# The second routed layer as one list of 47 tiles, with the shared expert behind its first nine

## The chip, the cores and the metric

The kernel runs on one core of a Trainium2 chip. The metric is device time in microseconds, the median of the runs: 534.43 us for the kernel before (three runs, 534.42 to 536.74). One instruction stream each drives PE (TensorE), ACT (ScalarE), DVE (VectorE), POOL (GpSimd) and SP (SyncE); they meet only at semaphores. SP's queue and POOL's queue start the DMAs.

## The reference

The input is four batches of 512 tokens of width 256: 2048 tokens, 16 tiles of 128. Half a routed feed-forward layer is added, then attention, then half of the same feed-forward layer once more.

```python
def _L0_ffn_ref(hidden_states, gate_w, expert_bias, ...):      # 16 experts, two per token
    scores = jax.nn.sigmoid(router_logits)                      # x @ gate_w
    _, selected = jax.lax.top_k(scores + expert_bias[None, :], K)
    top_scores = top_scores / (top_scores.sum(-1, keepdims=True) + 1e-20)
    shared = jax.nn.silu(x @ shared_gate_w) * (x @ shared_up_w) @ shared_down_w
    for e in range(E):
        gu = x @ experts_gate_up[e]
        g, u = jnp.split(gu, 2, axis=-1)
        routed = routed + comb[:, e:e + 1] * (jax.nn.silu(g) * u @ experts_down[e])
    return (shared + routed).reshape(b, s, h)
...
    x = x + 0.5 * _L0_ffn_ref(_layernorm(x, axis=-1), ...)      # FFN 1
    x = x + _L0_attn_ref(_layernorm(x, axis=-1), ...)           # per batch, 3 heads, all 512 x 512 scores
    x = x + 0.5 * _L0_ffn_ref(_layernorm(x, axis=-1), ...)      # FFN 2
```

## The kernel before

The whole x stays in SBUF (`x_sb`), and so do all weights. Each fp32 product is made of three passes over a high and a low part, so ACT copies a high part out of PSUM and DVE subtracts to get the low part.

A token goes to two experts. In FFN 2 the 4096 (token, expert) pairs lie in DRAM in `slab_dram`, one slab of rows for each expert. POOL writes them there with indirect DMAs (`slab_row`, L1879), one DMA for 128 tokens and one of their two choices. A tile is 128 rows of one slab. SP loads it (`load_row`, L2045), PE turns it (`turn`, L396), multiplies by the expert's gate and up weights (six matmuls), ACT takes silu (L1006), DVE multiplies (L1577), PE turns the result (L657), PE multiplies by the down weights (three matmuls) and ACT copies the output out (L1017); SP stores it to `y_dram` (L2072). `ffn` runs this as a pipeline: in step s, PE turns tile s, does gate and up of tile s-1, turns the hidden rows of tile s-3 and does the down product of tile s-4. Four row buffers hold loaded tiles. So SP can load tile n once tile n-4 has been turned.

A list of tiles must be known before SP and PE can index. DVE computes it from the counts of each expert (`tile_table`), PE brings it into one row (`pack_table`), DVE writes it (`write_table`), and SP and PE load registers from it. Attention runs batch by batch, and the routing of batches 0 to 2 is done beside it. Batch 3 is ready only when attention ends. So FFN 2 has two lists: one for batches 0 to 2, up to 39 tiles, and one for batch 3, up to 23 tiles; 62 steps that are always run. After each list's rows SP writes zeros behind each slab (`clear_rest`, L2057, 16 DMAs each time), so that the unused lanes of a last tile hold zeros.

Beside the steps of FFN 2, `late_front` on each engine does the routing of batch 3 (turns, router product, sigmoid, choice, ranks, slab addresses, eight slab stores) and brings batches 0 to 2 back: SP reloads their normed rows from `xn_dram`, PE turns 12 tiles (`return_tile`, L461), ACT and DVE split them. Those are the inputs of the shared expert, which is done for all four batches after the last tile (`shared_gu`, `shared_y`).

Last, POOL gathers each token's two outputs from `y_dram` (`gather_pair`, L1869, 32 indirect DMAs), DVE adds them into `x_sb` with their weights (`combine`, L1492), DVE adds the shared expert's output (`shared_sink`, L1258), and SP stores the output (`tail2`, L2109). The order on each engine is the order in which the code is written; there is no scheduler.

## Time and profile before

| | |
|---|---|
| median of 3 runs | 534.43 us (534.42, 534.43, 536.74) |
| span of the profiled execution | 536.0 us |
| PE, PEld, DVE, ACT, POOL busy | 466.7, 414.9, 350.9, 280.6, 255.1 us |
| attention's last matmuls end, first tile of FFN 2 is turned | 394.96 us, 396.24 us |
| last down product of FFN 2 ends | 510.89 us |

The page gives the profiled execution no time of its own besides its span. The span lies between the lowest and the highest of the three runs. "Idle before" names what an engine waited for and for how long. A group of rows with "x2" is two instructions whose spans may overlap.

### The profile page before, as it was taken

What the parts mean: (1) busy time and instruction counts of PE and PEld (TensorE: products, weight loads), DVE (VectorE), ACT (ScalarE), POOL (GpSimd) and SP (SyncE); (2) the same over time, 40 slices, a digit from 0 to 9 for tenths busy, and PEclk for the clock granted to TensorE, in tenths of its full rate; (3) what the DMA queues carried; (4) which work ended last, traced back from release to release, by engine and by line L of the source; (5) the groups of instructions that cost most, each with busy time, mean ns of one, the idle gap of its engine ahead of it and who ended that gap; (6) DMA issues with size and microseconds to landing.
All of it is one profiled execution on the core that took longest, in us unless ns stands there. A gap on an engine that the chain in (4) does not pass through costs nothing.

```text
span 536.0 us, 10796 instructions
## 1 busy us (share of the span) xinstructions
PE 466.7 (87%) x3155; PEld 414.9 (77%) x3155; DVE 350.9 (65%) x1048; ACT 280.6 (52%) x763; POOL 255.1 (48%) x262
## 2 busy tenths in 40 slices
PE   1566799999777999999999999999888999899985
PEld 1335688999666989988898988899777888898874
DVE  5469675565457655387466756756648677678766
ACT  3765266676533445445444544454446866566621
POOL 4357775565064753474337557373740022026571
PEclk9987599999999999999999999999989999999999
DMA  8743445665631200011002111030545477758755
GB/s 296 246 127 117 138 140 179 196 207 135 163 91 59 60 1 0 21 51 39 11 1 59 41 41 50 10 109 11 181 126 181 158 224 235 224 167 252 213 150 178
DMA packets 52263, 65.49 MB, mean 122 GB/s; under 512 B 7056, under 2 KB 45456, under 8 KB 52208
## 3 DMA queue, kind: packets, MB, share of 16 engines
q1 hardware_dynamic: 44928, 46.02, 26.8%
q0 software_dynamic: 6864, 18.75, 12.9%
q8 instruction: 29, 0.48, 0.4%
q14 instruction: 26, 0.21, 0.1%
q10 hardware_dynamic: 416, 0.02, 0.1%
HBM read 36.33 MB, written 28.44 MB: 121 GB/s over the span
## 4 chain that ended last, share of the span: by engine, by line
PE 43%; DVE 8%; DMA 6%; issue 4%; ACT 3%; SPq 2%; POOL 1%; DVEq 0%; ACTq 0%
PE bank L390 38%; DMA stage<-slab_dram 4%; PE bank L396 3%; DVE x_sb L1492 1%; DVE softmax_row L1743 1%; PE bank L420 1%; PE bank L657 1%; ACT v_sp L1143 1%; DVE x_sb L1603 1%; SPq L2072 1%; DVE v_sp L1757 1%; DVE raw L1194 1%; DMA late_pair<-y_dram,slot_i 1%; DVE stats L1175 0%; POOL e_sp L1957 0%
## 5 line engine op out<-in xcount | busy, mean ns | idle before, releaser
L1957 POOL TENSOR_TENSOR e_sp<-raw,e_sp 128x512 fp32r<-128x512 f32 x48 | 62.3, 1298 | 72.1 <-ACT e_sp L1114 71.7
L390 PE MATMUL bank<-v_sp,e_sp 128*128 128x256 f32 x576 | 77.2, 284 | 2.0 <-DVE x_sb L1603 1.9
L390 PEld LDWEIGHTS bank<-v_sp,e_sp 128*128 128x128 f32 x576 | 74.3, 191 | 5.7 <-issue 2.7
L390 PE MATMUL bank<-g_sp,xT 128*128 128x512 f32 x288 | 74.8, 395 | 0.1
L390 PE MATMUL bank<-w_hi,e_sp 128*128 (+1 forms) x234 | 62.5, 293 | 2.4 <-DVE e_sp L1242 1.0
L390 PE MATMUL bank<-w_hi,xt_late 128*128 x248 | 61.8, 311 | 0.6 <-DVE xt_late L1572 0.5
L1924 POOL DMA_INDIRECT raw<-xn_dram,gather_at x47 | 46.2, 983 | 31.7 <-PE bank L396 28.8
L390 PEld LDWEIGHTS bank<-g_sp,xT 128*128 128x128 f32 x288 | 51.7, 189 | 9.4 <-issue 0.2
L1135 ACT ACTIVATE raw<-bank,softmax_row 128x512 f32<-128x512 f32 x48 | 33.2, 692 | 48.6 <-DVE softmax_row L1743 48.2
L1568 DVE TENSOR_TENSOR e_sp<-bank,e_sp 128x128 fp32r<-128x128 f32 x109 | 31.5, 289 | 30.9 <-ACT e_sp L987 30.1
L1743 DVE TENSOR_REDUCE softmax_row<-bank 128x1 f32<-128x512 f32 x48 | 32.9, 685 | 28.1 <-PE bank L390 27.8
L1869 POOL DMA_INDIRECT late_pair<-y_dram,slot_i x32 | 31.0, 969 | 39.0 <-DMA y_dram<-raw 24.0
L390 PE MATMUL bank<-b_sp,xT 128*128 128x256 f32 x288 | 44.0, 289 | 5.1 <-DVE v_sp L1757 4.9
L390 PEld LDWEIGHTS bank<-w_hi,e_sp 128*128 128x128 f32 x234 | 43.9, 189 | 5.5 <-issue 3.2
L1006 ACT ACTIVATE raw<-bank 128x128 f32<-128x128 f32 x109 | 30.4, 279 | 32.8 <-PE bank L390 32.6
L1757 DVE SCALAR_TENSOR_TENSOR v_sp<-bank,softmax_row,v_sp 128x256 fp32r<-128x256 f32 x48 | 23.2, 484 | 35.9 <-ACT v_sp L1143 35.9
L390 PE MATMUL bank<-w_hi,xT 128*128 x188 | 46.1, 307 | 0.6 <-DVE xT L1572 0.5
L390 PEld LDWEIGHTS bank<-w_hi,xt_late 128*128 128x128 f32 x248 | 44.2, 196 | 1.6 <-issue 1.2
L390 PEld LDWEIGHTS bank<-b_sp,xT 128*128 128x128 f32 x288 | 38.0, 191 | 7.4 <-DVE v_sp L1757 6.9
L1862 POOL DMA_INDIRECT stage<-y_dram,slot_i x32 | 32.3, 1010 | 22.4 <-DMA y_dram<-stage 14.6
L1577 DVE TENSOR_TENSOR raw<-raw,bank 128x128 f32<-128x128 f32 x109 | 31.2, 286 | 15.1 <-ACT raw L1006 10.7
L390 PE MATMUL bank<-xT,a_sp 128*128 128x512 f32 (+1 forms) x156 | 36.0, 379 | 0.8 <-DVE xT L1512 0.7
(247 smaller groups left out, 1123.3 us busy)
## 6 DMA issues: line engine op xcount, KB each, us to landing
stage<-slab_dram SPq DMA_DIRECT2D x62, 128.0 KB
y_dram<-raw SPq DMA_DIRECT2D x62, 128.0 KB, 2.7
y_dram<-stage SPq DMA_DIRECT2D x47, 128.0 KB, 2.6
slab_dram<-stage SPq DMA_DIRECT2D x32, 128.0 KB
stage<-in_w_pack SPq DMA_DIRECT2D x6, 384.0 KB, 5.4
raw<-in_w_pack SPq DMA_DIRECT2D x6, 384.0 KB, 3.4
x_sb<-in_x SPq DMA_DIRECT2D x4, 512.0 KB, 7.8
xn_dram<-xn_all SPq DMA_DIRECT2D x4, 512.0 KB, 4.6
```

The source lines that it names most:

```text
L390: m = pe.matmul(dst, lhs[k][l], rhs[k][r], start=(first and k == 0 and i == 0), stop=(last and k == n - 1 and i == 2), skip_group_check=True)
L396: m = pe.transpose(dst[:, k * P:(k + 1) * P], src[:, k * P:(k + 1) * P], ident[:])
L1006: act.activation(h_buf[:, g % 2, :], bank[GU_BANKS[g % 2]][:, 0:F], ACT.Silu).then_inc(s_silu, 1)
L1135: act.activation(e32[:, i, :], bank[S_BANKS[i]][:], ACT.Exp, bias=row_max[:, i, :], accum_out=row_sum[:, i, :]).then_inc(s_exp, 1)
L1568: dve.tensor_tensor(ht_rows[:, v % 2, 1], bank[HT_BANK][:, 0:P], ht_rows[:, v % 2, 0].bitcast(F32), ALU.subtract).then_inc(s_hT_lo, 1)
L1577: dve.tensor_tensor(h_buf[:, g % 2, :], h_buf[:, g % 2, :], bank[GU_BANKS[g % 2]][:, F:GU], ALU.mult).then_inc(s_act, 1)
L1743: dve.tensor_reduce(row_max[:, i, :], bank[S_BANKS[i]][:], AX, ALU.max, negate=True).then_inc(s_max, 1)
L1757: dve.scalar_tensor_tensor(out=v_sp[:, i, 1, :], in0=bank[V_BANK][:, 0:H], scalar=row_inv[:, i, :], in1=v_sp[:, i, 0, :].bitcast(F32), op0 ...
L1862: pool.indirect_dma_start(pair_buf[:, n % PAIRS, :], None, y_dram[0:NI * P, :], at).then_inc(s_pair[n % PAIRS], 16)
L1869: pool.indirect_dma_start(late_pair[:, n % LATE_PLACES, :], None, y_dram[0:(SPLIT_TILE if t < LATE_T else TILES[1]) * P, :], at).then_inc( ...
L1924: pool.indirect_dma_start(row_buf[0][:, n % ROWS, :], None, xn_dram, bass.IndirectOffsetOnAxis(ap=gather_at[:, n:n + 1], axis=0)).then_inc ...
L1957: pool.tensor_tensor(e_sp[:, i, 1, :], e32[:, i, :], e_sp[:, i, 0, :].bitcast(F32), ALU.subtract).then_inc(s_e_lo, 1)
```

## The change

One list takes the place of two. The first nine tiles are full tiles of batches 0 to 2: of their 3072 pairs at most 16 x 127 can lie outside full tiles, whatever the routing, so at least nine tiles are full, and these need neither zeros nor batch 3. Then the shared expert of all four batches is done, two of its gate and up products within steps 9 and 10 of the nine tiles, the rest after them. Then 38 tiles follow that hold all that is left, 47 in all. `slab_dram` has one slab per expert, with room for all batches, and zeros are written once (17 DMAs).

Rows of `slab_dram` are 272 floats wide instead of 256: the 257th holds the number of the pair (choice and token), written by POOL into the source before each slab store (`mark`). POOL reads it back from each loaded tile (`keep_id`) and scatters the tile's output straight to the place of the pair in `pair_dram` (`scatter_y`), instead of SP's store to `y_dram`. SP then loads both outputs of 128 tokens with one plain DMA (`load_pair`), instead of two gathers. SP may load tile n only after `keep_id` of tile n-4. `combine` is no longer spread over the steps: all 32 stand behind FFN 2 on DVE.

The inputs of the shared expert for batches 0 to 2 are no longer turned a second time: SP stores the turned tiles that the router used (`xT_dram`) and loads them back (`reload_batch`), ACT copies the high part and POOL subtracts (`back_hi`, `back_lo`, 128x1024 each), batch 0 in attention's last batch and batches 1 and 2 in FFN 2's first steps. The routing of batch 3 stands earlier by some steps, and the weights of all batches are computed in the later steps of the second part.

```diff
+    FULL_TILES = (LATE_T * TOPK * P - E * (P - 1)) // P + 1
+    EARLY_TILES = LATE_T * TOPK + E - 1
+    TILES = (NI, NI)
     BASE = (0, NI)
-    DONE = (NI, NI + TILES[1])
-    STEPS = tuple(n + LAG for n in TILES)
-    SLAB_TILES = (LATE_T + 1, TB + 1)
-    SLAB = sum(SLAB_TILES) * P
-    SLAB_LATE = SLAB_TILES[0] * P
-    TABLE = ((0, 40, 40), (80, 104, 24))
-    LATE_PLACES = 8
-    PAIRS_FROM = 44
+    DONE = (NI, NI + NI)
+    STEPS = (NI + LAG, NI + LAG)
+    ROW = H + 16
+    SLAB = T + P
...
+    y_put_value = [pairs_read[j % PAIRS] + 16 * (j // PAIRS + 1) for j in range(NI)]
...
-            shared_gu(1, 0)
-            for b in range(B):
-                if b + 1 < B:
-                    shared_gu(1, b + 1)
-                shared_y(1, b)
+            ffn(1, late_front, 0, FULL_TILES)
+            shared_y(1, 0)
+            shared_gu(1, 2)
+            pack_table(True)
+            shared_y(1, 1)
+            shared_gu(1, 3)
+            shared_y(1, 2)
+            shared_y(1, 3)
+            ffn(1, lambda s: None, FULL_TILES)
...
+            def back_hi(b):
+                x = front_x[1][b]
+                act.wait_ge(s_back[b], 16)
+                act.copy(x[:, 0], x[:, 1].bitcast(F32)).then_inc(s_back_hi, 1)
...
+            def late_shared(s):
+                if s == 10:
+                    shared_mul(1, 0)
+                elif s == 11:
+                    shared_lo(1, 0)
+                elif s == 12:
+                    shared_mul(1, 1)
+
+            def late_weights(s):
+                if s == FULL_TILES + 8:
+                    run(routing_weights(1, 0, LATE_T))
+                elif s == FULL_TILES + 16:
+                    run(routing_weights(1, LATE_T, NT))
...
-            ffn(1, between2)
-
-            for t in range(EARLY_COMBINED, LATE_T):
-                combine(1, t)
-            shared_mul(1, 0)
-            shared_lo(1, 0)
-            shared_mul(1, 1)
+                late_shared(s)
+
+            ffn(1, between2, 0, FULL_TILES)
             shared_lo(1, 1)
+            write_table(True)
             shared_sink(1, 0)
-            combine(1, LATE_T)
             shared_mul(1, 2)
-            combine(1, LATE_T + 1)
             shared_lo(1, 2)
             shared_sink(1, 1)
             shared_mul(1, 3)
-            combine(1, LATE_T + 2)
             shared_lo(1, 3)
-            combine(1, LATE_T + 3)
             shared_sink(1, 2)
             shared_sink(1, 3)
+            ffn(1, late_weights, FULL_TILES)
+            for t in range(NT):
+                combine(1, t)
...
+            def mark(rows, n, new):
+                nonlocal marked
+                if new:
+                    pool.memset(rows[:, H + 1:], 0.0).then_inc(s_mark, 1)
+                pool.tensor_copy(rows[:, H:H + 1], pair_id[:, n:n + 1]).then_inc(s_mark, 1)
+                marked += 2 if new else 1
+                pool.wait_ge(s_mark, marked)
...
+                if k == 1:
+                    pool.wait_ge(s_slab[t % TB], 16 * (t // TB * TOPK + 1))
+                mark(src, k * NT + t, k == 0 and (t < TB or t >= LATE_T))
...
+            def back_lo(b):
+                x = front_x[1][b]
+                pool.wait_ge(s_back_hi, b + 1)
+                pool.tensor_tensor(x[:, 1], x[:, 1].bitcast(F32), x[:, 0].bitcast(F32), ALU.subtract).then_inc(
+                    s_back_lo, 1)
+
+            def keep_id(j):
+                pool.wait_ge(s_row_late[j % ROWS], row_value(j))
+                row = row_buf[1][:, j % ROWS, :]
+                pool.tensor_scalar(tile_id[:, j % (TOPK * NT):j % (TOPK * NT) + 1], row[:, H + 1:H + 2], float(j),
+                                   row[:, H:H + 1], ALU.mult, ALU.add).then_inc(s_id, 1)
+
+            def scatter_y(j):
+                pool.wait_ge(s_y_copy, BASE[1] + j + 1)
+                pool.wait_ge(s_id, j + 1)
+                pool.indirect_dma_start(pair_dram, bass.IndirectOffsetOnAxis(
+                    ap=tile_id[:, j % (TOPK * NT):j % (TOPK * NT) + 1].bitcast(U32), axis=0), y_buf[1][:, j % Y_BUFS, :], None).then_inc(
+                        s_pair[j % Y_BUFS], 16)
...
-            pool.wait_ge(s_row_norm, NT + TB)
-            for t in range(LATE_T, NT):
-                for k in range(TOPK):
-                    pool.wait_ge(s_xt, BASE[1] + SCATTER_FROM + SCATTER_EVERY * ((t - LATE_T) * TOPK + k))
+            for j in range(ROWS):
+                keep_id(j)
+            back_lo(1)
+            keep_id(4)
+            scatter_y(0)
+            keep_id(5)
+            scatter_y(1)
+            back_lo(2)
+            keep_id(6)
+            scatter_y(2)
+            keep_id(7)
+            keep_id(8)
+            scatter_y(3)
+            for k in range(TOPK):
+                for t in range(LATE_T, NT):
                     slab_row(t, k)
-            for t in range(NT):
-                gather_pair(1, t)
+            for j in range(4, FULL_TILES):
+                scatter_y(j)
+            for s in range(FULL_TILES, NI + LAG):
+                if s < NI:
+                    keep_id(s)
+                if s - LAG >= FULL_TILES:
+                    scatter_y(s - LAG)
...
                 if n >= ROWS:
                     sp.wait_ge(s_xt, BASE[1] + n - ROWS + 1)
+                    sp.wait_ge(s_id, n - ROWS + 1)
                 sp.dma_start(row_buf[1][:, n % ROWS, :], slab_dram[bass.ds(rows["at"][i % PER_LOAD], P), :]).then_inc(
                     s_row_late[n % ROWS], 16)
...
+            def load_pair(t):
+                if t in (0, LATE_T):
+                    for i, value in enumerate(put_by(EARLY_TILES if t == 0 else NI)):
+                        sp.wait_ge(s_pair[i], value)
+                if t == 0:
+                    sp.wait_ge(s_ssink, 2 * B + 8)
+                sp.dma_start(late_pair[:, t], pair_rows[t]).then_inc(pairs_loaded[t][0], 16)
...
+            rows = {}
+            for n in range(ROWS):
+                load_row(n, rows)
+            reload_batch(1)
+            reload_batch(2)
+            for n in range(ROWS, FULL_TILES):
+                load_row(n, rows)
+            clear_rest()
+            for n in range(FULL_TILES, NI):
+                load_row(n, rows)
+            for t in range(NT):
+                load_pair(t)
```

POOL, from the end of attention on, before. `slab_dram<-stage` are slab stores, `e_sp` the low part of attention's exponentials, `late_pair` the gathers.

```order
L1957 TENSOR_TENSOR e_sp<-raw,e_sp 128x512
L1879 DMA slab_dram<-stage,lane 36864x256 x2
L1957 TENSOR_TENSOR e_sp<-raw,e_sp 128x512
L1879 DMA slab_dram<-stage,lane 36864x256
L1957 TENSOR_TENSOR e_sp<-raw,e_sp 128x512
L1825 TENSOR_TENSOR rstd<-variance,columns 128x4
L1879 DMA slab_dram<-xn_all,lane 36864x256 x8
L1869 DMA late_pair<-y_dram,slot_i 128x256 x32
```

The same place now. `slot_i<-stage` is `keep_id`, `x_front` and `g_sp` with 1024 columns are `back_lo`, `pair_dram<-raw` is `scatter_y`.

```order
L2005 TENSOR_TENSOR e_sp<-raw,e_sp 128x512
L1887 COPY stage<-pair_id 128x1
L1903 DMA slab_dram<-stage,lane 34944x272
L2005 TENSOR_TENSOR e_sp<-raw,e_sp 128x512
L1846 TENSOR_TENSOR rstd<-variance,columns 128x4
L1926 TENSOR_SCALAR slot_i<-stage 128x1 x4
L1920 TENSOR_TENSOR x_front<-x_front 128x1024
L1926 TENSOR_SCALAR slot_i<-stage 128x1
L1932 DMA pair_dram<-raw,slot_i 10112x256
L1926 TENSOR_SCALAR slot_i<-stage 128x1
L1932 DMA pair_dram<-raw,slot_i 10112x256
L1920 TENSOR_TENSOR g_sp<-g_sp 128x1024
```

POOL now has work in the steps of the tiles, and the first outputs leave behind two `back_lo`. Further on, after the last of batch 3's slab stores, POOL now has:

```order
L1887 COPY xn_all<-pair_id 128x1
L1903 DMA slab_dram<-xn_all,lane 34944x272
L1932 DMA pair_dram<-raw,slot_i 10112x256 x5
L1926 TENSOR_SCALAR slot_i<-stage 128x1 x5
L1932 DMA pair_dram<-raw,slot_i 10112x256
L1926 TENSOR_SCALAR slot_i<-stage 128x1
L1932 DMA pair_dram<-raw,slot_i 10112x256
L1926 TENSOR_SCALAR slot_i<-stage 128x1
L1932 DMA pair_dram<-raw,slot_i 10112x256
```

Where eight slab stores and 32 gathers stood, there is one `keep_id` and one `scatter_y` per tile, each in the queue behind the other.

DVE at the end of FFN 2, before. L1492 is `combine`, the rows with 512 columns are the shared expert's.

```order
L1568 TENSOR_TENSOR e_sp<-bank,e_sp 128x128
L1492 SCALAR_TENSOR_TENSOR x_sb<-late_pair,weight,x_sb 128x256 x8
L1238 TENSOR_TENSOR bank<-bank,xn 128x512
L1242 TENSOR_TENSOR v_sp<-bank,v_sp 128x512
L1238 TENSOR_TENSOR bank<-bank,raw 128x512
L1242 TENSOR_TENSOR e_sp<-bank,e_sp 128x512
L1258 SCALAR_TENSOR_TENSOR x_sb<-bank,x_sb 128x512 x2
L1492 SCALAR_TENSOR_TENSOR x_sb<-late_pair,weight,x_sb 128x256 x2
L1238 TENSOR_TENSOR bank<-bank,xn 128x512
L1492 SCALAR_TENSOR_TENSOR x_sb<-late_pair,weight,x_sb 128x256 x2
L1242 TENSOR_TENSOR v_sp<-bank,v_sp 128x512
L1258 SCALAR_TENSOR_TENSOR x_sb<-bank,x_sb 128x512 x2
```

The same place now (L1608 and L1617 are the steps' own rows, L1532 is `combine`).

```order
L1612 TENSOR_TENSOR xt_late<-bank,xt_late 128x256
L1617 TENSOR_TENSOR raw<-raw,bank 128x128
L1608 TENSOR_TENSOR e_sp<-bank,e_sp 128x128
L1617 TENSOR_TENSOR raw<-raw,bank 128x128
L1608 TENSOR_TENSOR e_sp<-bank,e_sp 128x128 x2
L1532 SCALAR_TENSOR_TENSOR x_sb<-late_pair,weight,x_sb 128x256 x32
```

The shared expert's rows are gone from here, and all 32 of `combine` stand behind the last row of the steps.

## Rows read from the trace of the kernel before

**Rows 1.** Stretches: length, PE, PEld, DVE, ACT, POOL busy (xcount), PEclk, DMA share, GB/s.
```profile
340.00:396.20 56.20, 51.77 (x347) 46.53 (x346) 34.54 (x105) 25.03 (x57) 32.67 (x30) 1.00 0.27 90
396.20:415.25 19.05, 16.78 (x102) 14.60 (x103) 14.30 (x51) 11.79 (x32) 1.04 (x1) 0.82 0.53 161
415.25:511.00 95.75, 87.49 (x695) 81.02 (x693) 72.83 (x251) 64.11 (x225) 28.68 (x30) 1.00 0.70 211
511.00:536.00 25.00, 17.45 (x96) 14.79 (x96) 16.39 (x31) 4.92 (x9) 10.07 (x11) 0.96 0.51 158
```

**Rows 2.** The same for L657 alone, one transpose per tile.
```profile
419.90:433.00 13.10, 2.52 (x9) 1.18 (x9) 1.00 0.56 175
433.00:464.00 31.00, 4.73 (x17) 2.36 (x17) 1.00 0.72 232
...
478.60:505.20 26.60, 4.37 (x16) 2.26 (x17) 1.00 0.81 232
```

**Rows 3.** Waits from 390 to 515: us in total, times, longest.
```profile
PE bank L396 <- DMA stage<-slab_dram: 6.6, 8, 1.7
...
PE bank L657 <- DVE e_sp L1568: 3.4, 4, 1.3
```

**Rows 4.** Chain that ended last, 375 to 400: start, us, what.
```profile
390.90 2.43 DMA slab_dram<-stage,lane
...
394.02 2.18 DMA stage<-slab_dram
```

**Rows 5.** Timeline of POOL, 372 to 393: start, us, instruction [idle before].
```profile
378.34 0.97 POOL L1879 DMA_INDIRECT slab_dram<-stage,lane  x1 [0.30 <-issue]
...
382.40 0.99 POOL L1879 DMA_INDIRECT slab_dram<-stage,lane  x1 [0.16 <-issue]
```

**Rows 6.** Timeline of POOL near the program's start.
```profile
6.38 0.24 POOL L1835 TENSOR_SCALAR variance<-moments 128x4 f32<-128x4 f32 x1 [3.53 <-DVE moments L1218]
...
28.32 1.85 POOL L1819 TENSOR_TENSOR w_lo<-raw,w_hi 128x768 fp32r<-128x768 f32 x1 [6.73 <-ACT w_hi L869]
```

**Rows 7.** Timeline of ACT, 384 to 425.
```profile
416.24 1.28 ACT L1041 ACT_TABLE_LOAD   x1
```

**Rows 8.** Timeline of PE, 388 to 428: turns of the hidden rows.
```profile
418.36 0.30 PE L657 MATMUL bank<-ident,raw 128*128 128x128 f32 x1 [1.31 <-DVE e_sp L1568]
...
425.94 0.27 PE L657 MATMUL bank<-ident,raw 128*128 128x128 f32 x1
...
427.35 0.27 PE L657 MATMUL bank<-ident,raw 128*128 128x128 f32 x1
```

**Rows 9.** Timeline of SP's queue, 355 to 396.
```profile
379.23 10.48 SPq L2057 DMA_DIRECT2D slab_dram<-stage  x16
```

**Rows 10.** Chain that ended last, 440 to 500: the shortest and the longest row load.
```profile
458.27 2.07 DMA stage<-slab_dram
...
491.39 4.97 DMA stage<-slab_dram
```

**Rows 11.** DMA, 433 to 464: queues, then issues.
```profile
q1 hardware_dynamic: 6825, 6.21, 62.7%
q0 software_dynamic: 336, 0.92, 8.5%
...
slab_dram<-xn_all,lane POOLq DMA_INDIRECT x7, 3.0
```

**Rows 12.** Chain that ended last, 505 to 536.
```profile
510.26 0.63 PE bank L390 x3
510.91 0.38 ACT raw L1017
...
518.07 8.64 PE bank L390 x48
```

**Rows 13.** Timeline, 511 to 536.
```profile
520.64 13.89 SPq L2109 DMA_DIRECT2D out<-x_sb  x16
...
527.42 1.08 DVE L1492 SCALAR_TENSOR_TENSOR x_sb<-late_pair,weight,x_sb 128x256 f32<-128x256 f32 x2
```

629 lines of the change are left out of this document (307 added, 322 removed).

## The prediction

> **What bounds the kernel now.** I read the table of stretches first. Until attention ends, at 396.2 us, and from there on, PE is the busiest engine: 16.8 of 19.0 us in the first steps of FFN 2, 87.5 of 95.8 us in the rest of its steps, 17.5 of the last 25.0 us [rows 1]. So FFN 2 and its tail are 140 of the 536.0 us, and PE's work counts there. The count of turned hidden rows by stretch gives the pace of a tile: 9 in 13.1 us (1.46 us each) where nothing but row loads and output stores runs, 17 in 31.0 us (1.82) where zeros are written, 16 in 26.6 us (1.66) where the gathers run [rows 2]. The best single step is 1.41 us [rows 8]. The DMA share says why: 0.56, 0.72 and 0.81 in the same three stretches [rows 2]. The waits name row loads as what PE waited for most (6.6 us in 8 waits beside its weight loads), then DVE's split of the hidden rows (3.4 us in 4) [rows 3]. The chain gives the length of a row load where one ended last: 2.07 to 4.97 us, with nothing in the row's size to tell them apart [rows 10].
>
> **The change, part by part.** All is against the span, 536.0 us.
>
> *Attention's end.* Each slab store now has one tiny POOL instruction ahead of it. Two stores in a row stood 0.97 + 0.30 us apart; a store behind a computing instruction waits 0.16 us, and a tiny instruction takes 0.24 [rows 5, 6]. That is some 0.15 us more for each, and three instead of two stores now stand ahead of the third last low part, 1.3 us. The last store (2.43 us to land) and the first load (2.18 us) are the chain into FFN 2 [rows 4], so what POOL loses there is lost: +1.6 us, between 0 (POOL had gaps) and 3. `back_hi`, `back_lo` of batch 0 and the list's extra DVE instructions (16 of about 0.2 us) I take at nothing: in the 56.2 us up to 396.2, DVE was busy 34.5, ACT 25.0 and POOL 32.7 us [rows 1]. If that cover fails, it is 2.5 us of `back_lo` (1.85 us for 768 columns, so 2.5 for 1024 [rows 6]).
>
> *Steps 0 to 8.* They took 19.0 us [rows 1], batch 3's router product included. Gone are two DVE chains that held PE for the part of the 3.4 us that is not the 1.31 of [rows 8]: 1.5 taken. New within these steps are the turns of the scores and the ranks (0.7 us, estimated), ACT's change to sigmoid and back, 1.28 us for each table [rows 7], behind which PE stood 1.31 us and its step was 0.5 longer besides [rows 8] (+1.8), and two `back_hi` in ACT's queue (half a `back_lo`, 0.8 each of it felt: +1.6). Then a new wait: row 8 may be loaded only after `keep_id` of tile 4, which stands on POOL behind a `back_lo` of 2.5 us, which waits for ACT's step 5; with 2.2 us for the load it comes some 7.5 us after that step, and PE wants it after 4 to 5: +2 taken, 0 to 4. Sum 23.6 us.
>
> *From step 9 to the second list.* Two calculations run beside each other. PE: four batches of the shared expert, 17.3 us (48 matmuls, which are two batches, took 8.64 [rows 12]), the rest of steps 9 to 12, some 3.5 us, and 1 to 2 us of waits for ACT and DVE: 22. POOL and SP: addresses 2.5 us after the ranks, then eight stores at 1.45 us and 3.0 us for the last to land [rows 11]: 17; and 17 zero writes at 0.66 us (16 took 10.48 [rows 9]) = 11.1 us, which begin 5 us after the ranks, 2.5 us to land, then a register load and a row load, 3 us: 22 to 23. They are level; I take 23.1. What is late next if PE is ahead is the row load of tile 9.
>
> *The 38 tiles.* PE does 15 tiles fewer. The pace is set by PE (1.41) or by the loop over a row buffer: the output copy ends 0.4 us after the product [rows 12], POOL issues the scatter (0.99 us, 0.16 behind a computing instruction [rows 5]), does `keep_id` (0.24 [rows 6]), SP issues the load (0.66 [rows 9]), and it must land within four steps: 4 p = 2.45 + L. A load of 2.2 us gives 1.16, one of 3.2 gives 1.41, one of 4.97 gives 1.86. POOL's own work is 1.4 us per tile. DMA per tile falls: of 62.7% and 8.5% of 31.0 us, 48 plain transfers and 7 scatters took 0.40 and 0.38 us each of all engines [rows 11], so a load and a scatter are 0.8 us of 1.45, a share of 0.55, the share of the 1.46 stretch. I take 1.47 us: 38 tiles, 55.9 us, and the four steps behind them 3.2 us (estimated): 59.1. Bounds 1.41 and 1.86.
>
> The page on DMA of the Trainium skill (DMA: Bandwidth & Descriptors, Anatomy of one DMA) fits a transfer as about 2.0 us and its bytes over 436 GB/s. For a row tile that is an estimate of 2.3 us, and by it alone the loop would never be felt and the pace would be PE's, 2.3 us less in the sum. The trace agrees with it for the shortest row load, 2.07 us, and not for the longest, 4.97 [rows 10].
>
> *The tail.* Before, the last product ended at 510.9 us [rows 12] and 25.1 us followed. Now 32 `combine` follow. Two that depend on each other took 1.08 us [rows 13], so about 1.0 us per token tile, 16 us, from 0.8 us before the last product's end, and 2.2 us for the last store: +17.4. The DMA queues are the other calculation: from about 5.5 us before the end, 32 plain units of pairs, 16 of output at 0.41 us and 8 scatters at 0.38, 22.7 us at full share, 25 at 0.9: +19.5 to +20. I take 20.0. Bounds 17.4 and 23.
>
> The same page (Queues, rings and completion order) says that a DMA engine takes turns between the queues that have work. By it the last scatters do not stand behind the twelve pair loads already issued, and land about when they would alone; in the trace a scatter beside a busy plain queue took 3.0 us [rows 11]. If they stood behind, the last four pair loads would be some 4 us later.
>
> *Sum.* 396.2 + 1.6 + 23.6 + 23.1 + 59.1 + 20.0 = 523.6 us, 12.4 less than 536.0. The span is 1.6 us above the median of the runs; I take the difference to the median: 534.4 - 12.4 = 522.0 us.
>
> **The rivals.**
>
> A. *PE's pace and DVE's tail hold.* 1.41 us a tile (-2.3), the tail at 17.4 (-2.6), attention's end at +0.5 (-1.1): 516 us. For it speaks the single step of 1.41 us and a lower DMA share; against it that no stretch held it.
>
> B. *The second list is late.* If 17 zero writes and eight slab stores share the DMA engines badly, the zeros run at 1.0 instead of 0.66 us: +6, 528 us. Against it: they need 25 x 0.41 = 10 us of all engines.
>
> C. *POOL becomes the bound of the 38 tiles.* With 1.4 us of its own per tile it has nothing to spare. If scatters take 1.15 to 1.2 us instead of 0.99, the pace is 1.6: +4.9, 527 us.
>
> D. *Slower: the row loads land late.* Before, a load went out behind an earlier output store; now it goes out behind an earlier scatter and `keep_id`, two queues in a row. If a load takes 5.3 us instead of about 3, a step is 1.94 us: 33 steps x 0.47 = +15.5, 537.5 us. It cancels the whole gain from a load of 4.95 us on, which is the longest of the row loads seen [rows 10], and those were seen at a share of 0.8.
>
> E. *It doesn't do what it says:* the list has 47 steps in the code and PE's issue order, so 15 tiles do go; I give this nothing.
>
> **How the numbers follow.** Forecast 0.52 (its own range 517 to 527), A 0.17, B 0.13, C 0.09, D 0.09. The range that holds the time 8 times in 10 is 514 to 531: A and below it by 2, B and C and most of the way to D. A measurement tells 0.5%, 2.7 us, from no change: faster means under 531.8, slower over 537.1. Faster gets the forecast, A, most of B and C, 0.85; same 0.06, the upper ends of B, C and the lower half of D; slower 0.09.
>
> **What would show it.** In the new profile: 47 turns of hidden rows behind attention; the first turn of FFN 2 at about 398 us; a gap or none before PE's turn of tile 8; PE's shared products unbroken, with the first row of the second part at about 444.5 us; from there 38 turns 1.47 us apart, with waits for row loads of a few us in sum, and POOL at about 1.4 us busy a tile; last product at about 504 us; then DVE's `combine` in one row, with the DMA share above 0.85, and the end 20 us later. Wrong would be: a pace above 1.6 us with PE waiting for row loads (D) or for nothing but POOL (C); a gap of 5 us or more before tile 9 (B); a tail under 18 us (A); or attention's batch 3 longer by more than 3 us, since I have put only 1.6 there.

## The result, and the profile after

The changed kernel takes 532.1 us, median of 20 runs (529.8 to 535.0), the kernel before beside it 535.3 us: a ratio of 0.9947, 95% interval 0.993 to 0.9964. It is faster by 3 us, where 12.4 were forecast; the forecast of 522.0 us was wrong, and 532.1 lies above its range too. The profiled execution has a span of 532.4 us. Its stretches, cut where FFN 2's first row turn, the first turn of the second part, and the last output copy stand (columns as in [rows 1]):

```profile
340.00:400.84 60.84, 53.39 (x347) 47.70 (x346) 40.28 (x124) 26.17 (x58) 38.36 (x49) 0.97 0.17 60
400.84:449.10 48.26, 39.72 (x231) 33.89 (x232) 26.30 (x90) 22.67 (x54) 27.65 (x44) 0.89 0.45 151
449.10:511.10 62.00, 56.92 (x458) 53.99 (x456) 41.99 (x133) 42.26 (x152) 45.05 (x71) 1.00 0.54 165
511.10:532.40 21.30, 0.00 (x0) 0.00 (x0) 13.49 (x30) 0.02 (x1) 3.14 (x3) 0.55 0.83 277
```

The stretch up to FFN 2's first row turn is longer: 60.8 us where [rows 1] has 56.2. The 38 tiles take 62.0 us with a DMA share of 0.54, the low share that was expected, and with POOL busy 45.05 us, three quarters, where before it had 28.68 of 95.75. Before the first row turn DVE holds PE up. The chain that ended last, 386 to 391 us (start, us, what; its longest pieces):

```profile
387.32 1.97 DVE tile_of L1417
389.31 0.41 DVE stage L1227
389.89 0.48 ACT v_sp L1175
390.40 0.49 DVE v_sp L1779
390.94 0.58 PE bank L394
```

`tile_of` L1417 is an instruction of `list_rest`, and PE stood 3.48 us for the `v_sp` behind it. (An instruction of this size takes 0.17 us; what held this one is told in the last section.) The waits of PE from 380 us on (us in total, times, longest), beside [rows 3]:

```profile
PE bank L400 <- DMA stage<-slab_dram: 5.3, 4, 2.8
PE bank L394 <- DVE v_sp L1779: 3.9, 2, 3.5
PE bank L673 <- DVE e_sp L1608: 3.1, 4, 1.1
PE bank L394 <- DVE xt_late L1612: 2.0, 2, 1.1
PE bank L394 <- DVE v_sp L1268: 1.7, 1, 1.7
```

The 2.8 us is the row turn of tile 8, the new wait that was forecast at +2. In the 38 tiles PE's steps are mostly 1.40 us, and about 1.55 every fourth. Three are much longer: 2.67 and 2.21 us, where DVE computes the routing weights, and 2.99. Timeline of PE around the last of them (start, us, instruction, [idle before]); L673 turns hidden rows, L400 a row tile:

```profile
481.97 0.27 PE L673 MATMUL bank<-ident,raw 128*128 128x128 f32 x1
...
483.37 0.27 PE L673 MATMUL bank<-ident,raw 128*128 128x128 f32 x1
...
484.77 0.27 PE L673 MATMUL bank<-ident,raw 128*128 128x128 f32 x1
486.35 0.44 PE L400 MATMUL bank<-ident,stage 128*128 128x128 f32 x2 [1.31 <-DMA stage<-slab_dram]
487.76 0.27 PE L673 MATMUL bank<-ident,raw 128*128 128x128 f32 x1
```

PE waits for a row load whose buffer POOL hasn't given back. POOL at the same time and at the end:

```profile
470.42 0.26 POOL L1926 TENSOR_SCALAR slot_i<-stage 128x1 int32<-128x1 f32 x1
470.95 1.02 POOL L1932 DMA_INDIRECT pair_dram<-raw,slot_i  x1 [0.27 <-issue]
472.06 0.26 POOL L1926 TENSOR_SCALAR slot_i<-stage 128x1 int32<-128x1 f32 x1
472.59 1.02 POOL L1932 DMA_INDIRECT pair_dram<-raw,slot_i  x1 [0.27 <-issue]
...
500.79 1.02 POOL L1932 DMA_INDIRECT pair_dram<-raw,slot_i  x1 [0.16 <-issue]
502.29 1.02 POOL L1932 DMA_INDIRECT pair_dram<-raw,slot_i  x1 [0.16 <-issue]
...
513.84 1.00 POOL L1932 DMA_INDIRECT pair_dram<-raw,slot_i  x1 [0.30 <-issue]
```

Its pitch is 1.64 us while it stands 0.27 us ahead of a scatter, later 1.50. Either is more than PE's 1.40 to 1.45, so POOL falls behind until a buffer holds PE back, and its last scatter goes out at 513.84, 2.7 us behind the last output copy (511.1). The chain from there (start, us, what):

```profile
513.84 5.71 DMA pair_dram<-raw,slot_i
...
520.62 5.54 DMA late_pair<-pair_dram
526.18 0.50 DVE x_sb L1532
```

Added up against the forecast's own marks:

| | forecast | measured | miss |
|---|---|---|---|
| FFN 2's first row turn | 397.8 | 400.8 | +3.0 |
| from there to the first turn of the second part | 46.7 | 48.3 | +1.6 |
| from there to the last product's end (510.7) | 59.1 | 61.6 | +2.5 |
| tail | 20.0 | 21.7 | +1.7 |
| span | 523.6 | 532.4 | +8.8 |

Each row is one profile's; the control below, the same kernel again, has the first and the third miss and not the other two. The other 1.3 us of the 10.1 are the medians: before, span and median stood 1.6 us apart, after 0.3.

### The profile page after: what moved, and what is told of

Read it like the earlier page. It is cut to its first block, busy times and chain, and to the rows that moved or that the text cites. A ratio compares the mean times of both kernels' runs of the same rounds, so it can differ in the third digit from the quotient of the medians.

```text
span 532.4 us, 10109 instructions
## 1 busy us (share of the span) xinstructions
PE 442.9 (83%) x2951; PEld 393.2 (74%) x2951; DVE 335.4 (63%) x985; ACT 265.8 (50%) x706; POOL 299.2 (56%) x371
## 4 chain that ended last, share of the span: by engine, by line
PE 32%; issue 11%; DVE 9%; POOL 7%; DMA 4%; SPq 2%; ACT 1%; ACTq 0%; DVEq 0%; POOLq 0%
PE bank L394 30%; POOL pair_dram L1932 5%; POOL slot_i L1926 2%; SPq L2123 1%; DVE softmax_row L1765 1%; DVE x_sb L1532 1%; PE bank L400 1%; ACT v_sp L1175 1%; DMA pair_dram<-raw,slot_i 1%; DVE x_sb L1638 1%; DMA late_pair<-pair_dram 1%; DMA stage<-slab_dram 1%; PE bank L424 1%; DVE v_sp L1779 1%; DVE stats L1208 1%
## 5 line engine op out<-in xcount | busy, mean ns | idle before, releaser
L2005 POOL TENSOR_TENSOR e_sp<-raw,e_sp 128x512 fp32r<-128x512 f32 x48 | 62.4, 1299 | 68.7 <-ACT e_sp L1144 68.3
L1932 POOL DMA_INDIRECT pair_dram<-raw,slot_i x47 | 47.9, 1020 | 15.2 <-issue 9.6
L1608 DVE TENSOR_TENSOR e_sp<-bank,e_sp 128x128 fp32r<-128x128 f32 x94 | 27.3, 291 | 41.0 <-ACT e_sp L1013 40.7
L394 PE MATMUL bank<-w_hi,e_sp 128*128 x188 | 51.5, 297 | 1.2 <-DVE e_sp L1608 1.1
L394 PE MATMUL bank<-w_hi,xt_late 128*128 x188 | 47.1, 313 | 2.0 <-DVE xt_late L1612 2.0
L1030 ACT ACTIVATE raw<-bank 128x128 f32<-128x128 f32 x94 | 26.3, 280 | 29.4 <-PE bank L394 29.4
L394 PEld LDWEIGHTS bank<-w_hi,e_sp 128*128 128x128 f32 x188 | 35.9, 191 | 3.8 <-issue 2.6
L1617 DVE TENSOR_TENSOR raw<-raw,bank 128x128 f32<-128x128 f32 x94 | 27.0, 287 | 15.3 <-ACT raw L1030 11.0
L394 PEld LDWEIGHTS bank<-w_hi,xt_late 128*128 128x128 f32 x188 | 33.8, 198 | 3.1 <-issue 2.8
```

The source lines that it names most:

```text
L394: m = pe.matmul(dst, lhs[k][l], rhs[k][r], start=(first and k == 0 and i == 0), stop=(last and k == n - 1 and i == 2), skip_group_check=True)
L1030: act.activation(h_buf[:, g % 2, :], bank[GU_BANKS[g % 2]][:, 0:F], ACT.Silu).then_inc(s_silu, 1)
L1608: dve.tensor_tensor(ht_rows[:, v % 2, 1], bank[HT_BANK][:, 0:P], ht_rows[:, v % 2, 0].bitcast(F32), ALU.subtract).then_inc(s_hT_lo, 1)
L1617: dve.tensor_tensor(h_buf[:, g % 2, :], h_buf[:, g % 2, :], bank[GU_BANKS[g % 2]][:, F:GU], ALU.mult).then_inc(s_act, 1)
L1932: pool.indirect_dma_start(pair_dram, bass.IndirectOffsetOnAxis(ap=tile_id[:, j % (TOPK * NT):j % (TOPK * NT) + 1].bitcast(U32), axis=0), y ...
L2005: pool.tensor_tensor(e_sp[:, i, 1, :], e32[:, i, :], e_sp[:, i, 0, :].bitcast(F32), ALU.subtract).then_inc(s_e_lo, 1)
```

## The experiments

The runs form four groups, each on one chip beside the kernel before, which took 550.9 us there (group 1), 536.1 (2), 549.4 (3) and 537.1 (4). Groups 1 and 3 are one chip, slower for every kernel; the changed kernel itself was not run on it. Totals are therefore compared within a group. Positions are from the profiles, one for each run: **start** is the distance from attention's first row maximum to FFN 2's first row turn (before 225.3 us, after 230.0, control 229.9), **loop** that from the second turn of the second part to the last output copy (after 61.8).

**id_dve**, group 1.

```
 # DVE's step s, between the split of the row tile and the product of the hidden rows
+dve.wait_ge(s_row_late[s % ROWS], row_value(s))
+dve.tensor_scalar(tile_id[:, j], row[:, H+1:H+2], float(s), row[:, H:H+1], MULT, ADD)   # j = s % 32
 # pool, tiles 9 to 46
-keep_id(s)
 scatter_y(s - LAG)
```

> The changed kernel with keep_id of tiles 9 to 46 on DVE, behind the split of the row tile, instead of on POOL ahead of the scatter. Theory (POOL bounds the 38 tiles): in the changed kernel POOL's scatters stand 1.64 us apart for the first 19 and 1.50 for most of the rest, 1.02 of it the scatter's issue, 0.26 keep_id and 0.16 to 0.28 ahead of the scatter. Without keep_id they can stand 1.3 us apart; PE then sets the pace, at about 1.3 to 1.4 us, 0.2 less for each of 38 tiles: last product some 7 us earlier than at 510.7, POOL's last scatter within 1.5 us behind it instead of 3.1, time 522 to 525 us. Rival (the pace is set by the row loads' landing or by the share of the DMA engines, and POOL only follows): the scatters stay 1.5 to 1.6 us apart with PE waiting for row loads, time within 2 us of 532.1.

Measured 547.4 us, ratio 0.9928 (0.9898 to 0.9959). POOL now waits 33.0 us for ACT's output copies, so it has room, but the loop takes 69.3 us and the steps are mostly 1.6 to 1.9 us (median 1.74, in list_late and keep_first on the same chip 1.50 and 1.49): no gain, the theory missed. joined_id_pool below comes back to it.

**id_twice**, group 1.

```
 # pool, keep_id, tiles 9 to 46
+pool.tensor_scalar(fixed[:, 64+j:65+j], row[:, H+1:H+2], float(j), row[:, H:H+1], MULT, ADD)
 pool.tensor_scalar(tile_id[:, j], row[:, H+1:H+2], float(j), row[:, H:H+1], MULT, ADD)
```

> The changed kernel with a second, unused copy of keep_id's instruction on POOL for tiles 9 to 46, in front of the first. Theory (POOL bounds the 38 tiles): each tile is longer by one such instruction, 0.26 us and perhaps 0.05 beside it: pitch of the scatters 1.8 to 1.95 us, time 10 to 12 us longer, about 543. Rival (row loads or the DMA share bound the pace, POOL has slack): under 3 us longer, 532 to 535.

Measured 551.0 us. The scatters' pitch is 1.97 us and later 1.72, 0.22 to 0.33 more than without the copy, and PE waits for row loads 12 times instead of 4. But the loop is 72.1 us against 68.7 in list_late and 68.8 in keep_first, which share it: +3.4, not 10 to 12. POOL had slack on this chip: in list_late it waits 11.2 us for ACT's copies and 8.8 us for row loads.

**list_late**, group 1.

```
 # dve, previous_front (attention's end)
-yield from list_rest()
+yield; yield
 # dve, late_front: first half at step 0, second half at step 4 of FFN 2
+rest = list_rest(); next(rest)
 ...
+next(rest)
```

> The changed kernel with the 18 instructions of list_rest (the first call's list for the second part) moved on DVE from the last units of attention to the first steps of FFN 2. Theory (they hold v_sp's low part up, PE waits 3.48 us for DVE ahead of 390.9): that wait goes to under 0.5 us, FFN 2's first row turn comes 3 us earlier than at 400.8, time 529 us. Rival (POOL's marks and slab stores set attention's end anyway): PE's wait moves to e_sp's low part on POOL, the first row turn comes under 1 us earlier, time 531 to 532.

543.8 us, ratio 0.9816 (0.9767 to 0.9864). Counted from the first row maximum, the last one comes 5 us earlier, the first row turn only 1.6: start is 228.4, against 230.0 to 230.3 in the three others of this group. The wait for DVE is gone (0.8 us left) and one for POOL has come:

```profile
PE bank L394 <- POOL e_sp L2009: 2.8, 2, 1.8
PE bank L394 <- DVE v_sp L1783: 0.8, 2, 0.4
```

Theory and rival are each half right: `list_rest` costs about 1.6 us net, the rest is behind POOL.

**keep_first**, group 1.

```
-back_lo(1)
 keep_id(4)
+back_lo(1)
```

> The changed kernel with keep_id of tile 4 ahead of the low part back_lo of batch 1 on POOL instead of behind it, so that the load of row 8 doesn't wait for it. Theory (PE's 2.77 us at the row turn of tile 8 is this wait and lies on the path through the ranks, zero_at and the zero writes): the wait is gone, zero_at is ready 2 to 2.8 us earlier than at 428.8, time 529.5 us. Rival (other work of these steps, ACT's tables and DVE's choice, stands right behind): the wait turns up at another place and the time falls by under 0.7 us, 531.5 to 532.

538.7 us, ratio 0.9811 (0.9775 to 0.9846). From the first row turn to that of tile 8 it takes 16.8 us; the three others of this group take 19.3 to 19.9, the changed kernel 20.1. The wait is gone and 3 us come out of the path.

**control**, **id_dve_end** and **weights_early**, group 2. The control is the changed kernel.

> The changed kernel itself, unchanged, so that the other kernels beside it are read against it on one chip. On the first chip it took 0.9947 of the time of before. Theory (the pace of the 38 tiles is near a tie between PE's own 1.40 us steps and POOL's 1.5 to 1.64 us): with slower landings PE's turns of hidden rows show steps over 2 us every third tile from some tile on, as in list_late and keep_first, and few or none on a chip where landings are short. Rival (the chip matters only as a constant factor): the ratio and the pattern of steps are those of the first chip.

Measured 533.3 us, 0.9955 (0.9933 to 0.9976), the ratio of the result. Its loop has steps of 1.40 and 1.55 us, two for the weights and two over 2 us behind late row loads. list_late and keep_first, on the slow chip, have five and six more steps over 2 us, but there PE waited for row loads only 0.8 and 1.0 us in the loop and 3.8 us for DVE's `e_sp` in both; so more long steps came, as the theory had it, mostly not for its reason.

The control is also a second profile of the changed kernel. It meets the first row turn 3.0 us late against the forecast, when the 1.1 us by which its attention began later are taken off; then 46.6 us to the second part (forecast 46.7), 62.5 us to the last product (59.1) and a tail of 20.4 us (20.0). Attention's end and the 38 tiles are late in both profiles, the other two stages only in the first.

```
 # id_dve_end: dve, step s
-keep_id's instruction ahead of the product of the hidden rows
+the same behind it, at the step's end
```

> The changed kernel with keep_id of tiles 9 to 46 on DVE, now behind the product of the hidden rows at the end of DVE's step, where DVE stands idle 0.34 us in each step. In id_dve it stood between two instructions that PE waits for, and the steps grew from 1.40 to 1.75 us. Theory (PE's loop through DVE has slack only there, and POOL is then free): steps of 1.40 to 1.57 us with two exceptions for the routing weights, scatters within 1.5 us of their output copy to the end, last output copy 2 to 6 us earlier than in the control relative to the first turn of the second part, time 4 to 7 us under the control. Rival (any DVE instruction in the loop costs its 0.2 us, wherever it stands): steps of 1.6 us and more, time within 2 us of the control or above it.

```
 # weights_early: dve
 shared_lo(1, 1)
+run(routing_weights(1, 0, LATE_T)); run(routing_weights(1, LATE_T, NT))
 write_table(True)
 ...
-ffn(1, late_weights, FULL_TILES)
+ffn(1, lambda s: None, FULL_TILES)
```

> The changed kernel with both calculations of the routing weights on DVE moved from tiles 17 and 25 of the loop to the shared expert's stage, where DVE waits 4.4 us for the packed table. Theory (they hold PE's next hidden turn up: those two steps take 2.67 and 2.21 us instead of 1.40): both steps fall to about 1.4 to 1.5 us and nothing else moves; if POOL bounds the tiles behind, the 2.0 us do not reach the end and the time falls by under 1 us; if PE bounds them, it falls by 2 us. Told apart by the distance of the last scatter from the last output copy: it grows by 2 us in the first case and stays in the second.

id_dve_end: 530.5 us, 0.990 (0.9874 to 0.9925), 2.9 us under the control; loop 61.1 us against 62.7, no step above 1.8 but the two of the weights; the last scatter 1.3 us behind the last copy. On this chip the instruction costs nothing at the end of DVE's step. The gain stayed under the 4 to 7 us expected, since the weights' steps remain.

weights_early: 532.9 us, 0.4 under the control. The steps of 2.71 and 2.20 us became 1.4, but the 2.0 us were not gained, and the distance of the last scatter from the last copy grew by 0.4 us only (1.8 to 2.2), not by 2. The control had two more long steps, 2.22 and 2.77 us, behind late row loads; here there are three, 3.05, 2.79 and 2.26, the first with this wait, and POOL's pitch is the old 1.64 us:

```profile
471.72 0.44 PE L400 MATMUL bank<-ident,stage 128*128 128x128 f32 x2 [1.36 <-DMA stage<-slab_dram]
```

A faster PE only meets the late buffer sooner. The loop is 62.1 us; two profiles of one kernel, 61.8 and 62.7, are further apart than this gain.

**joined**, group 2: list_late, keep_first, weights_early and id_dve_end in one kernel.

> The changed kernel with four edits together: keep_id of tiles 9 to 46 at the end of DVE's step, keep_id of tile 4 ahead of POOL's back_lo, list_rest in FFN 2's first steps, the routing weights in the shared expert's stage. Theory (the misses are separate stalls that add up): attention's end 1.7 us earlier, the row turn of tile 8 2.8 us earlier, 2 us for the weights, 4 to 7 us for the loop and the last scatter: 9 to 13 us under the control. Rival (they hide each other, because zero_at and the zero writes set the start of the second part whatever comes before): 4 to 6 us under the control.

523.4 us, 0.9778 (0.9748 to 0.9808): 10.0 us under the control, as the theory had it. Its loop is 58.0 us.

It was run again in group 3, as joined_again, and in group 4, as joined_third. joined_again: 538.1 us, 0.9789 (0.9746 to 0.9831), but its steps are not the 1.40 us expected: median 1.58. joined_third: 522.6 us, 0.9736 (0.9675 to 0.9796), start 228.4 as expected. Stretches of joined_third, cut at the same events as above:

```profile
340.00:398.40 58.40, 51.19 (x342) 45.68 (x341) 35.75 (x106) 25.32 (x58) 38.20 (x49) 1.00 0.18 62
398.40:441.40 43.00, 35.97 (x232) 29.71 (x232) 32.63 (x121) 22.21 (x54) 25.77 (x40) 1.00 0.46 154
441.40:500.30 58.90, 56.67 (x456) 54.07 (x456) 43.56 (x156) 41.90 (x152) 35.54 (x38) 1.00 0.62 192
500.30:519.80 19.50, 0.00 (x0) 0.00 (x0) 13.15 (x30) 0.00 (x0) 2.07 (x2) 0.51 0.83 281
```

PE is busy 56.67 of 58.90 us in the loop and waits 1.1 us for row loads: it is PE that bounds the loop now. POOL has 0.44 us to spare ahead of each scatter, waiting for the output copy:

```profile
473.38 0.96 POOL L1944 DMA_INDIRECT pair_dram<-raw,slot_i  x1 [0.44 <-ACT raw L1043]
474.78 0.96 POOL L1944 DMA_INDIRECT pair_dram<-raw,slot_i  x1 [0.44 <-ACT raw L1043]
```

**joined_id_pool**, group 3, and **joined_id_pool2**, group 4: the same kernel, joined with `keep_id` left on POOL.

> joined with keep_id of all tiles back on POOL; the other three edits stay. Theory (with PE's stalls gone, POOL's 1.5 to 1.64 us a tile bind all the sooner): hidden turns over 2 us apart several times behind the first ten, last scatter 3 us behind the last output copy, time 4 to 6 us over joined_again. Rival (most of joined's gain came from the edits ahead of the second part, POOL's share is small): under 2 us over it.

> joined_id_pool again. On its first chip the hidden turns of joined itself were 1.70 us apart, as before of 549 us, so that it could not tell where keep_id is better. Theory for a chip where joined's turns are 1.40 to 1.55 us apart (before near 535 us): keep_id on POOL makes the turns over 2 us apart several times, the last output copy 2 to 4 us later from the first turn of the second part and the last scatter 2 to 3 us behind it, time 3 to 6 us over joined_third. On a chip with turns of 1.7 us: within 2 us of it, as in the first run. Rival: no difference on either chip.

On the slow chip it took 535.8 us, joined_again 538.1: no loss, the theory missed. On the fast one it took 528.4 us against 522.6, +5.8, with a loop of 61.2 us against 57.6, steps of 2.91 and 2.81 us, waits for row loads of 3.7 us in 5, and the last scatter 2.2 us behind the last copy. So the second form of the theory held where joined's turns are 1.40 us.

On the slow chip joined's longer turns (mean 1.71 us in joined_again) come with `keep_id` on DVE, and go with it. The median step is 1.41 us in joined_id_pool, 1.49 and 1.50 in keep_first and list_late, all with it on POOL; it is 1.58 to 1.74 in id_dve, joined_again, joined_stores and joined_few_pairs, all with it on DVE. Turns of hidden rows, joined_id_pool and then joined_again:

```profile
456.07 0.27 PE L673 MATMUL bank<-ident,raw 128*128 128x128 f32 x1
457.47 0.27 PE L673 MATMUL bank<-ident,raw 128*128 128x128 f32 x1
458.87 0.27 PE L673 MATMUL bank<-ident,raw 128*128 128x128 f32 x1
```

```profile
459.81 0.27 PE L674 MATMUL bank<-ident,raw 128*128 128x128 f32 x1
461.70 0.30 PE L674 MATMUL bank<-ident,raw 128*128 128x128 f32 x1 [0.33 <-issue]
463.52 0.27 PE L674 MATMUL bank<-ident,raw 128*128 128x128 f32 x1
```

On the fast chips the same instruction on DVE left the steps at 1.40 us. Why it didn't on this one is open.

**joined_stores**, group 3.

```
-(15, 16, 17, 18, 18, 19, 20, 21)[n]
+(15, 15, 17, 17, 19, 19, 21, 21)[n]
```

> joined with the eight slab stores of batch 2 at other places on POOL: in pairs behind the low parts of e_sp, none ahead of them (slots 15, 15, 17, 17, 19, 19, 21, 21 instead of 15, 16, 17, 18, 18, 19, 20, 21). In joined PE waits 1.74 and 0.34 us for POOL's e_sp at attention's end, behind seven stores of 1.47 us each. Theory (three stores in a row ahead of one low part make this wait, their order and not their number): the wait falls by 1 us or more and FFN 2's first row turn comes about 1 us earlier. Rival (POOL is full there, 8 stores of 1.47 us and 4 low parts of 1.3 in 19 us): the wait moves to the last low part or to the first row load, which goes out behind the last store; no gain, or 1 us lost.

538.3 us against 538.1, start 228.4 against 228.5: nothing. The waits for `e_sp` are 2.8 us against 2.6. The rival holds.

**joined_few_pairs**, group 3. The eight pair loads of token tiles 4 to 11 are left out, and their combines read the pairs of tiles 0 to 3.

```
 for t in range(NT):
-    load_pair(t)
+    if not TB <= t < LATE_T: load_pair(t)
```

> joined without the loads of eight of the twelve early pair tiles (token tiles 4 to 11); their combines stand and take the pairs of token tiles 0 to 3 instead. Theory (the last scatters land late, 5.4 us against a median of 2.9, because twelve pair loads of 256 KB run beside them): the last scatter lands in about 3 us, the pair loads of token tiles 12 to 15 go out 2.4 us earlier and land in about 3 instead of 4 us. DVE's 32 combines stand in one row in joined, so the end stays within 0.5 us: DVE bounds the tail, the DMA queues have 3 to 4 us to spare. Rival (the output stores at the end wait for the DMA engines, share 0.96 in the last 10 us): the end comes 1 to 3 us earlier though DVE's row is as long.

537.3 us against 538.1. The last pair load is issued 4.0 us behind the last scatter instead of 6.3, so the last scatters do land 2.3 us later beside the pair loads. From the last output copy to the end it is 16.5 us against 17.9. To the last combine it is 13.5 and 13.6 us, the same; 1.2 us come from what follows, the output stores. The theory had the end within 0.5 us, the rival 1 to 3 us earlier: these 1.4 us are the rival's lower end. DVE's 32 combines bound most of this tail, the queues the end.

**marks_half** and **marks_twice**, group 4, against joined_third (522.6 us, start 228.4).

```
 # marks_half, rows of batches 1 and 2. dve, row_again(t):
+dve.tensor_copy(slab_src[:, t % TB, H:H + 1], pair_id[:, t:t + 1])
 # pool, slab_row(t, k):
-mark(src, k * NT + t)
+if k == 1: mark(src, k * NT + t)
 # marks_twice: pool, slab_row(t, k)
+mark(src, k * NT + t)
 mark(src, k * NT + t)
```

> joined with the pair number of a row's first copy, in batches 1 and 2, written by DVE behind the row's normalisation instead of by POOL ahead of the store: POOL has four marks fewer at attention's end. Theory (POOL is full there and each mark costs it 0.19 us and the longer gap ahead of the store, 1.47 against 1.28 us a store): first row turn 0.6 to 0.8 us earlier against attention's start, 227.7 to 227.9 us. Rival (PE's waits there come from the half clock or from the order of the work, POOL has slack between stores): under 0.2 us.

> joined with each mark of batches 1 and 2 done twice on POOL: eight more at attention's end, some 0.45 us each with the wait for it. Theory (POOL is full from its first store of batch 2 on): the first row turn comes 2.5 to 3.6 us later, 231 to 232 us behind the first row maximum, and PE's wait for e_sp grows by as much. Rival (POOL has slack there): under 1 us later.

marks_twice: 526.6 us, start 232.3, +3.9 where 2.5 to 3.6 were expected. The edit doubles sixteen marks, eight of them in batch 1's stores, and an extra mark took 0.24 us (0.18 and 0.06 ahead of it), not 0.45: 3.8 us of POOL's time in sum, all of it felt. Half is felt before batch 2's first store, which goes out 2.3 us later: `back_lo` of batch 0 ends 2.1 us later and holds a DVE instruction up to there, 3.06 us instead of 2.04. PE's wait for `e_sp` grew by 0.5 us only (2.8 to 3.3), that for DVE's `v_sp` by 1.4 (0.8 to 2.2). marks_half: 524.1 us, start 229.7, +1.2 where -0.7 was expected: theory and rival both missed. Its last row maximum already comes 1.1 us later, PE's wait for DVE's `v_sp` is 1.2 instead of 0.8 us: DVE has no slack either. What batch 2's eight marks cost in sum was not measured by taking them all away; from the pitch of two stores (1.48 us with a mark, 1.27 without [rows 5]) it is an estimate of 1.6 us.

## Why the prediction was wrong

*The mechanism held.* 15 tiles are gone, the DMA share of the loop fell to 0.54, the row loads landed mostly within 2.0 to 3.3 us where rival D needed 5.3, zeros took 11.5 us (B), PE's step is 1.40. The Trainium skill (DMA: Bandwidth & Descriptors, Anatomy of one DMA) gives the fit that the prediction sets beside its sum for DMAs of GpSimd's queue; row loads are SP's, so it is no more than a neighbour of these numbers. Each of the four misses has the same sign, and together they are seven tenths of the gain; by the control two of them, attention's end and the 38 tiles, belong to the kernel. One sign of being wrong that the prediction named came: attention's batch 3 longer by more than 3 us.

*Attention's end, +4.6 instead of +1.6.* The step that failed is "`back_hi`, `back_lo` of batch 0 and the list's extra DVE instructions I take at nothing: in the 56.2 us up to 396.2, DVE was busy 34.5". Spare time is not enough: what counts is what the moved instructions hold up. The list stands in the last third of that stretch, where DVE went from 9.89 to 12.66 us busy of 16. Before the change DVE was no fuller there than on average (62% and 61%), but POOL was: 12.50 of 16 us against 32.67 of 56.2. Stretch 376 to 392 us, before and then after:

```profile
376.00:392.00 16.00, 14.28 (x97) 12.62 (x97) 9.89 (x30) 7.46 (x17) 12.50 (x13) 1.00 0.57 190
```

```profile
376.00:392.00 16.00, 11.69 (x76) 10.13 (x75) 12.66 (x48) 4.86 (x11) 11.51 (x17) 0.95 0.13 48
```

list_late and joined give `list_rest` 1.4 to 1.7 us, about the size of its one long wait for POOL (1.8 us, last section). The remaining 3.1 sit behind POOL; marks_twice shows that what is added there is felt. The traces of before and list_late, counted from the first row maximum, say where: POOL's last slab store goes out at 219.9 and 222.9 us, 3.0 later, and the first of the last eight at 206.1 and 207.6, 1.5 later already. This store waits for DVE's `lane`, which is ready 1.1 us later, because `back_lo` of batch 0 held an instruction of its chain. Before, then after (L1320 is L1297 before; x2 are two, the first of which took 0.23 and 2.05 us):

```profile
366.74 0.36 DVE L1297 TENSOR_TENSOR route<-expert_no,top_at 128x64 f32<-128x64 f32 x2
377.05 0.98 POOL L1879 DMA_INDIRECT slab_dram<-stage,lane  x1 [0.30 <-DVE lane L1324]
```

```profile
366.46 2.40 POOL L1920 TENSOR_TENSOR xT<-xT 128x1024 fp32r<-128x1024 f32 x1
366.90 2.19 DVE L1320 TENSOR_TENSOR route<-expert_no,top_at 128x64 f32<-128x64 f32 x2
378.43 1.00 POOL L1903 DMA_INDIRECT slab_dram<-stage,lane  x1 [0.28 <-POOL stage L1887]
```

The 1.6 forecast for POOL fits the eight marks alone; 1.1 of the other 1.5 is by these rows `back_lo`, which the prediction took at nothing. On POOL itself it was covered (POOL waited 2.63 us behind it). No run took it away, so this is read and not shown; the order of the stores isn't it (joined_stores).

*Steps 0 to 8 and the second list, +1.6.* The new wait was 2.8 us, forecast at 2, and keep_first takes it out whole. The shared expert and the zero writes were not level here: the load of tile 9 had landed at 446.4 us, and PE came to it at 449.10 (control 447.2 and 448.51), so PE was the longer of the two. The clock adds to it: within these 48.3 us PE had three stretches at the lower level (last section), the control one, and the control took 46.6 us.

*The 38 tiles, +2.5.* The step that failed is the pace of 1.47 us, with no term for two things. The routing weights on DVE, 1.3 and 0.8 us of PE's path, I never named. And "POOL's own work is 1.4 us per tile" counted the gap ahead of a scatter as 0.16 us where it was 0.27 for half the tiles, and nothing for the 0.1 us behind: 1.64 and 1.50. That is rival C, held at 0.09, with its 1.6 us and a milder effect, since the backlog had to fill the buffers first. The two hide each other: on the fast chips the loop is 62.7 and 61.8 us with both, 62.1 without the weights, 61.1 without `keep_id` on POOL, 57.6 and 58.0 without either. Against the control they bring 0.6 and 1.6 us singly, together 4.7 to 5.1. The last two have the edits ahead of the loop as well; so has joined_id_pool2, with `keep_id` on POOL, and it stands at 61.2. With both gone, PE's steps beat the forecast's 1.47 us: 58.2 us in joined from the first turn to the last product, against 59.1.

*The tail, +1.7, in the control +0.4.* The 20.0 us counted the DMA queues from the last product on; the last scatter was issued 2.7 us late and landed in 5.7 us, not 3.0. The Trainium skill's page on DMA (DMA: Bandwidth & Descriptors, Queues, rings and completion order) has it that queues take turns on an engine; the runs lie between the two readings: beside eight pair loads more a scatter lands 2.3 us later, not behind them all, and not as if alone. Without POOL's backlog the tail is 18.4 us in joined and 19.9 in joined_third, one kernel, so part of the miss varies from run to run. It ended inside the bounds of 17.4 and 23.

## What to carry to other kernels

"Hidden behind other work" is not settled by a busy share. Look at every engine in the very stretch in which the moved instructions stand (POOL was at 78% there, 58% on average), and then at what waits for the engine that gets them: an instruction of 0.2 us on DVE stood 2 us beside POOL's, and the chain behind it ran late. Small costs taken at nothing or too low ate seven tenths of a gain that was otherwise right. When an edit gives one engine a small fixed task per tile, compare its full pitch, gaps included, with the pace that the bounding engine will have afterwards. Where two engines are within some per cent of each other, edit both before judging: either edit alone shows little. And profile the same kernel twice before explaining a miss of a stage: two of the four misses here were not there the second time.

## What was unexpected on the chip

**The place in a DVE step.** The same 0.2 us instruction made steps of 1.6 to 1.9 us between two instructions that PE waits for (id_dve) and cost nothing at the step's end (id_dve_end). But joined_again has it at the step's end on id_dve's chip, and its steps are nearly as long (median 1.58 against 1.74; the loop 71.8 us against 69.3). So the chip and not the place makes most of the difference; whether the place matters is not shown.

**DVE stands still beside POOL.** `tile_of` L1417 adds two columns that lie in SBUF. In the changed kernel it took 1.96 us and ended when POOL's `e_sp` did (387.98 to 389.25):

```profile
386.97 0.99 POOL L1903 DMA_INDIRECT slab_dram<-stage,lane  x1 [0.28 <-POOL stage L1887]
387.04 0.06 DVE L1415 MEMSET top<- 128x1 f32 x1
387.13 0.15 DVE L1416 TENSOR_SCALAR tile_of<-columns 128x1 f32<-128x1 f32 x1
387.32 1.96 DVE L1417 TENSOR_TENSOR tile_of<-tile_of,tile_at 128x1 f32<-128x1 f32 x1
387.98 1.27 POOL L2005 TENSOR_TENSOR e_sp<-raw,e_sp 128x512 fp32r<-128x512 f32 x1
389.31 0.41 DVE L1227 TENSOR_SCALAR stage<-x_sb,moments,rstd 128x256 f32<-128x256 f32 x1
```

The same stands in all seven profiles with `list_rest` at this place (1.95 to 1.97 us), and `back_lo` of batch 0 held L1320 for 2.04 or 2.05 us in the same way in 16 of the 17 profiles that have it, and for 3.06 in marks_twice. The Trainium skill (SBUF — State Buffer, SBUF: two separate sides) says that a DVE instruction with two SBUF inputs and a GpSimd operation that reads SBUF need the same pair of ports, and that whichever starts first has it for its whole instruction while the other blocks. The trace agrees for L1320, which began 0.44 us behind `back_lo` and ended with it, and for the end of L1417; but other such DVE instructions ran in their 0.18 us beside POOL's issue of a store, and L1417 stood from 0.66 us before `e_sp` began, which the rule doesn't say. No busy share shows such a wait: DVE counts as busy in it.

**The granted clock.** In the changed kernel PE ran at the lower level, 1.2 GHz, in four stretches of 3.4 us between 390 and 439 us; each set in during a wait of PE or within 1.1 us behind one (3.5, 1.1, 2.8 and 1.7 us). The control had two such stretches, the kernel before one of 6.8 us at 397. joined had 13.6 us of it between 394.5 and 435.5 us, joined_third none, though it has waits of 1.8, 1.5 and 1.7 us too; from the first row maximum to the second part they took 274.3 and 271.4 us. So the lower level can make 2.9 us between two runs of one kernel, and a wait doesn't always bring it.

**A slower chip.** The kernel before took 549 to 551 us on it. There ACT's silu sometimes starts late although PE's product has ended by the profile: 1.1 us in joined_again's loop (470.9 us), 3.7 us at the shared expert's last batch in list_late (450.4 us), where keep_first had no such gap. In both the semaphore that PE's product raises went up only at 470.87 and 450.37 us, and ACT started 0.02 us behind it; so it is the signal that is late, or the product's end, which the profile models. Median landings of a scatter were 4.0 to 5.2 us instead of 2.7 to 3.0. Why is open.
